# A four-layer recurrent network on one core: layer 3's gate, LayerNorm and penalties of the next chunk are made during this chunk, and constant products are placed at the first maxima

## The reference

```python
for each layer:
    xn = layernorm(x)
    s  = attention(xn)
    g  = silu(feed_forward(xn))
    x  = x + s * g
```

```python
g       = sigmoid(xn @ Wg + bg)                 # one gate for each token; Z_I by row, Z_J by column
res     = (1 - Z_I) * maximum(1 - Z_I - Z_J, 0) + Z_I * minimum(1 - Z_I + Z_J, 1)
scope   = clip(power(256 - 2, 1 - g) + 2 - abs(i - j), 1e-32, 1)
log_pen = log(maximum(res * scope, 1e-32))
scores  = q @ k.T / sqrt(8) + log_pen
```

## Time and profile before

| what | us |
|---|---|
| median of 3 runs (4226.57 to 4237.04) | 4228.34 |
| the profiled execution, its own time | 4234.82 |
| its span, first to last instruction | 4233.2 |
| TensorE busy (74% of the span) | 3121.1 |
| VectorE busy (57%) | 2419.7 |
| ScalarE busy (42%) | 1756.8 |
| GpSimd busy (28%) | 1192.0 |
| mean granted TensorE clock, as a share of full speed | 0.826 |

### The profile page before, as it was taken

The page is one execution under the profiler, slowest core; times in us unless marked ns, Lnnn a source line. Parts: engine busy times, 40 slices in busy tenths (PEclk is TensorE's granted clock), DMA queues, the critical chain, the costliest instruction groups (busy, mean ns, idle before and its releaser), DMA issues. The chain is left out here.

```text
span 4233.2 us, 54691 instructions
## 1 busy us (share of the span) xinstructions
PE 3121.1 (74%) x20450; PEld 1694.0 (40%) x20450; DVE 2419.7 (57%) x3405; ACT 1756.8 (42%) x3556; POOL 1192.0 (28%) x878
## 2 busy tenths in 40 slices
PE   6788888887343778888767678676786867768687
PEld 3444444444131333444334344343443434434344
DVE  2344444444263778778855665556665565656655
ACT  2333333333132555556434434344343444535344
POOL 0000000000232454445543243332433324233242
PEclk7888888888655889999878879688796887969779
DMA  2000000000121222333300000000000000000001
GB/s 95 8 7 5 3 7 7 7 7 5 65 92 50 69 74 75 92 88 88 84 18 6 9 1 6 8 6 9 1 6 8 6 9 1 6 8 6 8 1 8
DMA packets 82171, 112.05 MB, mean 26 GB/s; under 512 B 9920, under 2 KB 47296, under 8 KB 81344
## 3 DMA queue, kind: packets, MB, share of 16 engines
q1 hardware_dynamic: 76608, 98.31, 7.7%
q0 software_dynamic: 5376, 11.02, 1.1%
HBM read 82.55 MB, written 26.74 MB: 26 GB/s over the span
## 5 line engine op out<-in xcount | busy, mean ns | idle before, releaser
L370 ACT ACTIVATE l_PT<-PB 128x512 f32<-128x512 f32 x512 | 277.9, 595 | 542.0 <-PE PB L281 542.0
L281 PE MATMUL PB<-l_QM,l_KP 32*128 32x256 f32 x2048 | 375.0, 496 | 131.6 <-DVE l_QM L419 76.0
L1412 POOL TENSOR_TENSOR l_ST<-l_ST,l_CT 128x1024 f32<-128x1024 f32 x128 | 316.4, 2472 | 354.3 <-DVE l_ST L1351 354.3
L408 DVE TENSOR_REDUCE keep_MXP<-PB 128x4 f32<-128x1024 f32 x256 | 301.3, 1219 | 109.1 <-PE PB L254 109.1
L1351 DVE TENSOR_TENSOR_SCAN l_ST<-l_DA,l_DB 128x1024 f32<-128x1024 f32 x128 | 355.6, 2778 | 4.4
L281 PEld LDWEIGHTS PB<-l_QM,l_KP 32*128 32x128 f32 x2048 | 242.7, 244 | 258.7 <-ACT l_PT L370 98.6
L704 POOL MEMSET l_KV<- 128x4 f32 x8 | 0.8, 104 | 941.3 <-POOLq L109 941.3
L1563 POOL TENSOR_TENSOR l_PT<-l_PT,l_PEN 128x512 f32<-128x512 f32 x168 | 213.1, 1290 | 186.0 <-ACT l_PT L370 186.0
L1345 DVE TENSOR_TENSOR l_DB<-PB,l_BT 128x1024 f32<-128x1024 f32 x128 | 155.3, 1213 | 137.5 <-PE PB L1111 137.5
L1274 ACT ACTIVATE l_DA<-PB,keep_aneg 128x510 f32<-128x510 f32 x256 | 161.1, 683 | 160.2 <-DVE l_ST L1351 83.4
L295 PE MATMUL PB<-l_PT,keep_VT 128*32 128x256 f32 x2048 | 187.6, 529 | 35.5 <-POOL l_PT L1563 25.6
(11 more groups left out here) (419 smaller groups left out, 6771.5 us busy)
## 6 DMA issues: line engine op xcount, KB each, us to landing
l_WB<-in_w2f_dram SPq DMA_DIRECT2D x80, 320.0 KB, 3.0
l_WB<-in_w2f_dram SPq DMA_DIRECT2D x80, 258.0 KB, 2.7
l_XR<-xs_mid SPq DMA_DIRECT2D x80, 64.0 KB, 1.8
ys_mid<-l_YO SPq DMA_DIRECT2D x80, 64.0 KB, 2.8
s_mid<-keep_S SPq DMA_DIRECT2D x17, 256.0 KB, 2.0
w3fs<-in_w3f_dram SPq DMA_DIRECT2D x1, 3127.0 KB, 18.1
keep_XI<-in_x_dram SPq DMA_DIRECT2D x9, 256.0 KB, 3.1
x_mid<-keep_X SPq DMA_DIRECT2D x9, 256.0 KB, 3.1
```

What stands on the lines that cost most here:

```text
L281: last = nc.tensor.matmul(PB[:, 4 + u % STBANKS, kt * SEQ:(kt + 1) * SEQ], b.KP[rows, a, i, k0:k0 + 128], b.QM[rows, n % 2, :], start=True ...
L370: nc.scalar.activation(b.PT[:, u % PSLOTS].rearrange("p k q -> p (k q)"), PB[:, 4 + u % STBANKS, :], ACT.Exp).then_inc(s.exp_done, 1)
L408: nc.vector.tensor_reduce(dst[:, 2 * pair:2 * pair + 2, :, 16 + n % 2], PB[:, 2 * pair:2 * pair + 2, :].rearrange("p r (t k) -> p r t k", ...
L1412: nc.gpsimd.tensor_tensor(b.ST[:, g % RING], b.ST[:, g % RING], b.CT[:, k % 2, :].unsqueeze(1).broadcast_to([128, 2, T]), ALU.mult).then_i ...
```

## The change

Layer 3 now works one chunk ahead. A new block, layer3_prepare, stands before the loop and makes the gated x, its LayerNorm, the gates and the penalties of chunk 0. These lie in buffers of their own (h.X, h.XN, h.GA, h.GU, h.PEN and others). In the loop the attention block starts with the projections from h.XN. Between its batches, and at its end, it makes the gated x, the LayerNorm and the raw gates of the next chunk; the mixing of expert rows and the products that add to x are GpSimd's now. The feed-forward block makes the penalties out of the gates, all on VectorE and ScalarE, spread over its second layer. GpSimd now weighs three tiles in the first batch too. Loads and gathers run two chunks ahead.

Where layer 0 calls the attention (no `ahead`), 11 constant products stand behind the first batch's scores; in layer 3 there are 6, after four transposes. The formula of the penalties is arranged in fewer operations.

```diff
+FIRST_MAX = 11
+NEXT_MAX = 6
+NEXT_TOKENS = 6
@@ att_tensor
         if masked:
-            pe.wait_ge(s.weighed_dve, NR + 2 * j + 1)
-            pe.wait_ge(s.weighed_pool, (NR - 1) * (2 * j + 1))
+            pe.wait_ge(s.weighed_dve, 2 * j + 2)
+            pe.wait_ge(s.weighed_pool, (NR - 1) * (2 * j + 2))
...
     scores(0)
+    if ahead:
+        ahead(0)
+    else:
+        keep_warm(nc, c, PB, FIRST_MAX)
...
@@ att_vector
-        for r in range(NR) if n == 0 else (NR - 1,):
-            u = NR * n + r
-            dve.wait_ge(s.exp_done, u + 1)
-            pt = b.PT[:, u % PSLOTS]
-            nc.vector.tensor_tensor(pt, pt, b.PEN[:, 2 * batch(n)[1]:2 * batch(n)[1] + 2, :], ALU.mult).then_inc(s.weighed_dve, 1)
+        u = NR * n + NR - 1
+        dve.wait_ge(s.exp_done, u + 1)
...
-        if masked and n == 0:
-            before(1)
-            weigh(0)
+        if ahead:
+            ahead(n)
@@ layer3_attention, TensorE
-                pe.wait_ge(s.y_mixed, 1)
...
-                ln_tensor(nc, pe, s, c, c.X[:], PB)
-                keep_warm(nc, c, PB)
-                pe.wait_ge(s.xn_ready, 1)
...
+                att_project(nc, pe, s, c._replace(XN=h.XN), w, PB)
+                def ahead(part):
+                    if part == 0:
+                        pe.wait_ge(s.y_gated, 1)
+                        turn_tokens(nc, c, PB, 7).then_inc(s.yT_ready, 1)
+                        pe.wait_ge(s.v_copied, 1)
+                        keep_warm(nc, c, PB, NEXT_MAX, 4)
+                        pe.wait_ge(s.y_copied, 1)
+                    elif part == 1:
+                        pe.wait_ge(s.x_ready, 1)
+                        nc.tensor.matmul(PB[:, 2, :], c.centre, h.X[:], start=True, stop=True).then_inc(s.ln_centred, 1)
+                    elif part == 2:
+                        pe.wait_ge(s.ln_square, 1)
+                        nc.tensor.matmul(PB[:, 3, :], c.mean, c.lnsq[:], start=True, stop=True).then_inc(s.ln_var, 1)
+                    else:
+                        pe.wait_ge(s.xn_ready, 1)
+                        pe.wait_ge(s.exp_done, NR * BATCHES)
+                        ahead_gates(nc, h, w, PB).then_inc(s.gate_ready, 1)
@@ layer3_attention, GpSimd
+                gate_tokens(nc.gpsimd, c, r, it + 1, link).then_inc(s.y_gated, 1)
+                nc.gpsimd.tensor_copy(c.X[:], h.X[:]).then_inc(s.kept, 1)
+                nc.gpsimd.tensor_copy(c.XN[:], h.XN[:]).then_inc(s.kept, 1)
+                pool.wait_ge(s.y_copied, 1)
+                nc.gpsimd.tensor_tensor(c.lnc[:], c.SI0[:], c.Y[:], ALU.mult).then_inc(s.product, 1)
+                for n in range(BATCHES):
+                    if n == NEXT_TOKENS:
+                        pool.wait_ge(s.gate_sigmoid, 1)
+                        link(nc.gpsimd.tensor_tensor(c.lnc[:], c.lnc[:], c.gb[:], ALU.mult))
+                        nc.gpsimd.tensor_tensor(h.X[:], c.X1[:], c.lnc[:], ALU.add).then_inc(s.x_ready, 1)
...
@@ the penalties, on VectorE, in the feed-forward block
+def gate_products(nc, h, sq, link):
+    gates = slice(sq * SEQ, (sq + 1) * SEQ)
+    for t in (2 * sq, 2 * sq + 1):
+        nc.vector.scalar_tensor_tensor(out=h.T2[:, t, :], in0=h.AJ[:, gates], scalar=h.GI[:, t:t + 1], in1=h.GA[:, gates],
+                                       op0=ALU.add, op1=ALU.mult)
+        last = nc.vector.scalar_tensor_tensor(out=h.T1[:, t, :], in0=h.AJ[:, gates], scalar=h.NI[:, t:t + 1], in1=h.AJ[:, gates],
+                                              op0=ALU.add, op1=ALU.mult)
+    link(last)
+def penalty(nc, c, h, k, link):
+    sq, step = divmod(k, 5)
...
+    if step == 0:
+        link(nc.vector.tensor_tensor(pen, c.dist.rearrange("p (t q) -> p t q", q=SEQ), two(h.PJ), ALU.add))
+    elif step == 1:
+        link(nc.vector.tensor_tensor(t2, t2, two(h.GA), ALU.min))
+    elif step == 2:
+        link(nc.vector.scalar_tensor_tensor(out=t1, in0=t1, scalar=0.0, in1=t2, op0=ALU.max, op1=ALU.add))
+    elif step == 3:
+        link(nc.vector.scalar_tensor_tensor(out=pen, in0=pen, scalar=1.0, in1=t1, op0=ALU.min, op1=ALU.mult))
+    else:
+        link(nc.vector.tensor_scalar(pen, pen, 1e-32, None, ALU.max))
@@ layer3_ffn, ScalarE
+                    if l == 0:
+                        link(nc.scalar.activation(h.GU[:], h.GA[:], ACT.Abs))
+                        link(nc.scalar.activation(h.GU[:], h.GU[:], ACT.Exp, scale=-1.0))
...
+                        if l == 1 and i == 1:
+                            act.wait_ge(s.gu_ready, 1)
+                            gate_powers(nc, c, h, link).then_inc(s.gi_ready, 1)
...
+                    if l == 0:
+                        act.preload_act_table_set(LN)
+                        nc.scalar.activation(h.GU[:], h.GU[:], ACT.Ln, bias=c.one).then_inc(s.ga_logged, 1)
                     act.preload_act_table_set(EXP_LN)
@@ layer3_ffn, VectorE (all for l == 1)
+                        gate_argument(nc, h).then_inc(s.gu_ready, 1)
...
+                        if l == 1 and i == 1:
+                            dve.wait_ge(s.gi_ready, 1)
+                            gate_negated(nc, h, link)
+                        elif l == 1 and i >= 2:
+                            gate_products(nc, h, i - 2, link)
...
+                        if l == 1 and m in (2, 4, 6):
+                            penalty(nc, c, h, m // 2 - 1, link)
+                    if l == 1:
+                        for k in (3, 4, 5):
+                            penalty(nc, c, h, k, link)
                     dve.wait_ge(s.o_ready, l + 1)
...
+                        for k in (6, 7):
+                            penalty(nc, c, h, k, link)
                     ln_vector(nc, dve, s, c, b.HN[:], PB, link, l).then_inc(s.hn_ready, 1)
+                        for k in (8, 9):
+                            penalty(nc, c, h, k, link)
@@ layer3_ffn, SyncE and GpSimd
+                load_gated(nc, sp, c, it + 2, x_mid, s_mid, s.next_loaded)
-                nc.gpsimd.tensor_copy(r.places[:], r.idx[:, :, bass.ts(it + 1, TT)]).then_inc(s.places_copied, 1)
+                nc.gpsimd.tensor_copy(r.places[:], r.idx[:, :, bass.ts(it + 2, TT)]).then_inc(s.places_copied, 1)
@@ network
+        layer3_prepare(nc, c, v3, r2, soft, h, x_mid, s_mid, ys_mid, PB)
         with nc.Fori(0, chunks) as it:
```

301 lines of the change are left out of this document (197 added, 104 removed).

## The result

The changed kernel takes **4002.99 us** (median of 4 runs, 3987.59 to 4016.88), the one before 4227.45 beside it (4203.07 to 4237.04). The ratio is 0.9476, 95% interval 0.9423 to 0.953: faster by 5%. The forecast was 3975, 28 us too low. Of the 247.2 us between the two profiled executions (4234.82 and 3987.59), 93.0 come from layers 0 and 1, 195.4 from layer 3's loop, the new block takes 40.8, and 0.4 go elsewhere. The profiled execution is the fastest of the four.

What follows compares the result with a forecast made beforehand. Waits and low clock, with no engine full, were taken as the bound. Layer 3's turns -224, new block +43 and layer 0 -75 took 4234.8 to 3979 us; 3975 was said, range 3880 to 4100.

Steps and rivals of the forecast that it cites:

- start to first turn: Layer 3, turn's start to first maxima turned: from 29.0 to about 10.7 us, taken as 18 us saved per turn.
- first to last turn: Layer 3's attention loop: stall goes, two of seven steps at low clock, 58.6 to 43 us, 15.5 saved per turn.
- end of attention: Layer 3's attention end: gate products +1, clock held longer -1, so 0 per turn, bounds -3.5 to +2.
- feed-forward: Layer 3's feed-forward, second layer: VectorE's negation, products and penalty steps add 5.5 us per turn, bounds +3 to +9.
- the new block, once: Block before layer 3's loop, running the whole chain unhidden: +43 us once, 35 to 50.
- layers 0 and 1, in all: Layer 0's attention: eleven constant products fill the 2.48 us wait and hold the clock, -75 us; layer 1 stays.
- the three loop steps: Penalty steps in the second feed-forward layer's score loop: 0.7 us each, 1.4 in all; at 1.75 each, 3.2 more per turn.
- Table loads: ScalarE after the first layer's last Gelu: one more load and a logarithm, 2.0 us inside a 4.18 us wait, costing nothing.
- rival 2: Layer 0's constant products change nothing and all else is as forecast: 4047 us, chance 0.15.
- Rival 1: The clock holds everywhere, in layer 3's loop and layer 0: 3876 us, chance 0.12.
- rival 3: Neither layer 3's nor layer 0's attention loop holds the clock: about 4160 us, chance 0.10.
- Rival 4: Feed-forward loses its clock, +25 us per turn: 4360 us with rival 3 (chance 0.05), about 4170 with the forecast.

Runs made afterwards that it cites:

- e9: The changed kernel again, no edit, on another chip; ratio 0.9379 to the kernel before, 3947.76 us.
- e6: The changed kernel without the six constant products behind layer 3's first scores; ratio 0.9601 to the kernel before, 4039.26 us.
- e3: The changed kernel with the second feed-forward layer's eight 256-column products and six penalty steps moved later; ratio 0.9234 to the kernel before, 3872.2 us.
- e8: The changed kernel with the edits of e3 and e4 together; ratio 0.9343 to the kernel before, 3939.58 us.
- e1: The changed kernel without the eleven constant products behind layer 0's first scores; ratio 0.9544 to the kernel before, 4010.36 us.
- e2: The kernel before, with only eleven constant products added behind layer 0's first attention scores; ratio 0.9849 to the kernel before, 4141.63 us.
- e11: The changed kernel with 24 constant products in the second feed-forward layer's TensorE wait; ratio 0.9398 to the kernel before, 3952.99 us.
- e4: The changed kernel with ScalarE's last norm of each feed-forward layer ahead of the first exponentials; ratio 0.9466 to the kernel before, 3986.89 us.

## Why the prediction came out right, and which terms were off

The mechanism came out: the start, the stall and the low clock at both first maxima are what the time was in. For the clock the runs with and without the products show it; for the start and the stall it is read from the profiles, and no run takes one of them back alone. The closeness of the total is in part luck. The profiled execution took 3987.6 where the sum gave 3979: layer 3's loop gave 29 us less than forecast, layers 0 and 1 gave 18 more, and the new block took 2 less.

Per turn of layer 3, in us, mean of eight turns:

| term | forecast | first profile | e9 |
|---|---|---|---|
| start to first turn | -18 | -15.9 | -16.2 |
| first to last turn | -15.5 | -20.4 | -22.1 |
| end of attention | 0 | -1.1 | -1.0 |
| feed-forward | +5.5 | +13.0 | +9.1 |
| sum | -28 | -24.4 | -30.2 |
| the new block, once | +43 | +40.8 | |
| layers 0 and 1, in all | -75 | -93.0 | -56 (turning line) |

**Start.** The five groups of projections were as thought, 7.4 us with half of them at low clock, but TensorE's first one starts 3.0 us after GpSimd's first instruction, a gap that my 10.7 left out.

**Attention loop.** The chance of a full clock was sized too low: 43 forecast, 38.2 and 36.5 in the mean. The falls in mid-loop, on which I put two low steps, are mostly gone. They didn't go with the 9.5 us stall: e6 has no stall, its loops start low, and they fall twice more. In e9, whose loops start at full clock, six of eight have no fall. So the falls went where the low start went; why a loop that starts low falls again isn't shown. The missing stall alone doesn't hold the clock either: without the six constant products e6 needs 49.5. Whether the products would have helped beside the stall was not tried.

**Feed-forward.** This is the mis-sized term: 5.5 forecast with bounds of 3 and 9, 13.0 and 9.1 measured. "Eight products of 256 columns at 0.43" had the price of work beside an idle GpSimd. Four of the eight ran beside its rotations and took 1.49, so the two groups take 7.45 instead of 3.6. At like clock all of it shows: the second layer's projections take 28.6 in e9 and 21.4 in e3, both starting low, and 26.9 and 19.7 where the first profile and e8 start at full clock, 7.2 in each pair. The low start adds 1.7 more in every turn of e9. In the first profile another 3.6 came from the first layer, mostly from the late copies shown at e9; e9 has none of them. The score loop took 2.5 and 2.1 instead of 1.4.

I had rows for this, and used them at the wrong place. The trace of before has 256-column operations of VectorE beside GpSimd's two-input ones, the nearest thing to the eight products, and they take three times 0.43:

```profile
2960.39 1.43 DVE L1449 TENSOR_SCALAR l_T<-l_AJ,l_GI 128x256 f32<-128x256 f32 x1
```

Instead I weighed the pair of the earlier trace rows, and read it wrongly. During the 0.68 GpSimd did not wait: it ran a one-input operation (L1456), and during the 1.75 a two-input one (L1457). I charged the risk to the three loop steps, which took 0.69 in all eight turns. There VectorE starts 0.04 us first, and GpSimd's scaling beside it takes 1.54 instead of 1.04. The order of the starts isn't the rule, though. In e3 the first product also starts 0.04 us ahead of a scaling, and there VectorE pays and GpSimd doesn't, in all eight turns:

```profile
2723.63 1.36 DVE L1514 SCALAR_TENSOR_TENSOR ahead_T<-ahead_AJ,ahead_GI,ahead_GA 128x256 f32<-128x256 f32 x1
2723.68 1.04 POOL L2060 TENSOR_TENSOR l3f_PP<-l3f_PP,l3f_RS 128x512 f32<-128x512 f32 x1 [0.49 <-DVE l3f_RS L1996]
```

The Trainium skill's rule that was weighed there (GPSIMD Engine Reference, section 1, Specifications) names the contention. For the products and the rotations the rows agree: both engines are slower beside each other. That section doesn't say who pays, and that decided the sum.

**Table loads.** Nothing, as forecast by the row of 1.28: ScalarE still waits 2.14 us for TensorE after both loads. The estimate by the Trainium skill's 2.66 (ScalarE: Activation LUTs, What ACT_TABLE_LOAD costs) is contradicted again; the logarithm starts 0.01 us after the first of them, at 2694.62 behind 2693.33 + 1.28.

**Layer 0.** -93 in the profile stands outside the bound of -85, and -56 in e9 on the other side of -75. In layer 0's attention alone it is -82.5 and -69.2, on both sides of -75; the rest of layers 0 and 1 gave 10 and took 13, which no term foresaw. The eleven products do what was said (rival 2, that they change nothing, is refuted by e1 and e2). What was wrong is that the low turn 1 of before, 22 us of the term, was taken as a property of the kernel.

Rival 1 (the clock holds everywhere) is close for the attention and wrong for the rest; rival 3 falls with the 1.00 windows. Rival 4, the feed-forward losing its clock, happened in small, and the prediction had named it as a sign of being wrong. The second layer's scores run at 0.85, of which e11 won no time back, and the projections ahead of them start at 0.57 in e9, which costs 1.7 us a turn.

Open: which turns lose the clock in mid-loop, and why e4 and e8 do so more often than e9. The same code gives 35.7 or 46.6 us within one execution. In the first profile the turn of 46.6 turns its first maxima 14.0 us after its start, the four of 35.7 after 13.6 to 14.3.
